# Two GpSimd drains left out at the end of a graph network, and the wait for the last outputs behind a flag load

## The chip, the cores and the metric

The kernel runs on one core of one Trainium2 chip. The metric is device time in microseconds (us) of one execution. The profile is of one execution; its span runs from the first recorded instruction to the last, and the device time of the same execution is a little longer. Engines are called PE (TensorE), DVE (VectorE), ACT (ScalarE), POOL (GpSimd) and SP (SyncE).

## The reference

Two graph networks over 6250 nodes of 64 features and 200,000 edges, each added to its input and followed by a layer normalisation:

```
edge_index = jnp.stack([src, dst])
x = _layernorm(x + sage(sage(x) -> relu))          # mean over incoming edges, two layers
x = _layernorm(x + L1(x, src, dst, edge_attr_16))  # three message layers, batch norm between them
```

```
m   = concatenate([x[dst], x[src], edge_attr]) @ W.T + b
agg = segment_sum(m, dst, num_segments=n)
h   = relu(agg)            # after layers 0 and 1: relu(batchnorm(h))
```

The output is `out`, 6250 rows of 64 float32 values.

## The kernel before

The kernel first builds a dense count matrix of the edges (`build`), and then, in `layers`, multiplies node features by it five times. Each of these propagations is one call of `propagate` with p = 0 to 4, inside a block of its own; after p = 2 and p = 3 a second block holds the batch normalisation. A propagation works through 13 blocks of nodes (NB, 512 nodes each, the last one short). For each of them PE sums in PM (L1325), DVE scales into S and F, PE applies the weights (PH, L1543 and L1544) and turns the result (PG, L1570). In p = 4 DVE then adds it to R and normalises it (`norm`, L1636 to L1645) into the tile `dd`, and POOL writes `dd` to `out` with one DMA for each of the 13 (`write`, L1474 and, for the last, L1477). The DMAs count up two semaphores in turn, `s_o[0]` and `s_o[1]` (named o0 and o1 in the program, numbers 196 and 197), by 16 each.

Order within an engine is the order in which the code is written. Between the engines there are semaphores inside a block, and a barrier of all five engines at each block's end. In the barrier each of PE, DVE, ACT and SP executes a drain and adds one to a gather semaphore; POOL executes a drain of its own, waits until four have been gathered, and then adds four to a release semaphore for which the others wait. All of this has the line of the `with nc.Block()`: L1001 for the propagations, L1035 for the last block.

At the end of p = 4 POOL waits until all its output DMAs have landed:

```
        if p == 4:
            g.wait_ge(s_o[0], 16 * 7)
            g.wait_ge(s_o[1], 16 * 6)
```

The closing block (from L1035) is a fallback. During p = 4 DVE has written a one-word `flag` (L1731), which says whether the count matrix was trustworthy. Each engine loads it into a register (`value_load`: L1038 on SP, L1046 on POOL, L1054 on DVE, L1062 on PE, L1070 on ACT) and branches. With the flag at 0, as here, each jumps over the code of the whole slow path (a second version of everything, `slow`) to the barrier that ends the closing block, and the program is over. `propagate` is also called for parts of this slow path, with its parameter `block` an object of class `Stage`, and then its variable `slow` is true.

Of the kernel before, what the change touches and what calls it, by code (L numbers as in the profile page):

```python
# [205 lines left out]
def blk(b):  # L206
    return 512 if b < NB - 1 else LASTW
# [36 lines left out]
def gnn(nc, ins, out):  # L244
    ctx = ExitStack()
    with ctx:
# [40 lines left out]
        }  # L287
        build(nc, ins, m)
        layers(nc, ins, m, out)


# [644 lines left out]
def layers(nc, ins, m, out):  # L936
    ctx = ExitStack()
    with ctx:
        def sb(name, shape, dt=f32):
            return ctx.enter_context(nc.sbuf_tensor(name, shape, dt))  # L940

        def ps(name, shape, dt=f32):
            return ctx.enter_context(nc.psum_tensor(name, shape, dt))

        def sem(name):
            return ctx.enter_context(nc.semaphore(name))

        t = {
            "Ares": m["Ares"],
            "Aring": m["Aring"],  # L950
            "S": sb("S", [128, 2, 512]),
            "rc": sb("rc", [128, 2, 512]),
            "cnt": sb("cnt", [16, NP // 16]),
            "hT": sb("hT", [128, 2, 512]),
            "dd": sb("dd", [128, 2, 4, 64]),
            "sq": sb("sq", [128, 2, 4, 64]),
            "st": sb("st_", [128, 2, 4, 4]),
            "bst": sb("bst", [64, NB, 6]),
            "bag": sb("bag", [64, 8]),
            "PM": [ps(f"PM{i}", [128, 512]) for i in range(3)],  # L960
            "PH": [ps(f"PH{i}", [128, 512]) for i in range(2)],
            "PG": [ps(f"PG{i}", [128, 4, 128]) for i in range(2)],
            "PB": ps("PB", [64, 512]),
            "gi": sb("gi", [128, 1], i32),
            "gd": sb("gd", [128, 1], i32),
            "gf": sb("gf", [128, 1]),
            "msg": sb("msg", [128, 64]),
            "junk": sb("junk", [128, 13 * SW // 4], u8),
            "dsum": sb("dsum", [128, 8, 4]),
            "csum": m["csum"],  # L970
            "s_sr": [sem(f"s_sr{i}") for i in range(len(SUMS))],
            "s_rb": [sem(f"s_rb{i}") for i in range(len(FACTORS))],
            "s_fin": sem("s_fin"),
            "s_xp": [sem(f"s_xp{i}") for i in range(len(GIVEN))],
            "fl": sb("fl", [1, 16]),

            "s_ar": [[sem(f"s_ar{i}_{h}") for h in range(2)] for i in range(2)],
            "s_mm": sem("s_mm"),
            "s_ea": sem("s_ea"),
            "s_cl": sem("s_cl"),  # L980
            "s_cr": sem("s_cr"),
            "s_cd": sem("s_cd"),
            "s_ck": sem("s_ck"),
            "s_xt": sem("s_xt"),
            "s_bp": sem("s_bp"),
            "s_again": sem("s_again"),
            "s_rd": sem("s_rd"),
        }


        t["acc"] = t["hT"][:].rearrange("p a b -> p (a b)").bitcast(u16)[:, 0:13 * SW // 2]
        sets = [{}, {}, {}]

        def pick(k):
            def get(name):
                if name not in sets[k]:
                    sets[k][name] = sem(f"q{k}_{name}")
                return sets[k][name]
            return get
        for p in range(5):  # L1000
            with nc.Block() as block:  # L1001
                if p == 0:
                    setup(nc, ins, m, t, list, block)
                propagate(nc, ins, m, t, p, pick(p % 2), out, lambda: [*sets[1 - p % 2].values()], block)
            if p in (2, 3):
                with nc.Block() as block:
                    normalise(nc, m, t, p, pick(p % 2), block)
        once = [x for x in t.values() if type(x) is type(t["s_mm"])]
        slow = [*restart(nc, ins, m, t, [*sets[0].values(), *sets[1].values(), *once]), Stage()]
        general(nc, ins, m, t, -1, pick(2), slow[-1])  # L1010
        slow.append(Stage())
        setup(nc, ins, m, t, lambda: list(sets[2].values()), slow[-1])
        for p in range(5):
            slow.append(Stage())
            general(nc, ins, m, t, p, pick(2), slow[-1])
            slow.append(Stage())
            propagate(nc, ins, m, t, p, pick(p % 2), out,
                      lambda p=p: [*sets[2].values(), *sets[1 - p % 2].values()], slow[-1])
            if p in (2, 3):
                slow.append(Stage())  # L1020
                normalise(nc, m, t, p, pick(p % 2), slow[-1])
        s_meet, s_go = sem("s_meet"), sem("s_go")

        def meet(engine, k):

            if engine is nc.gpsimd:
                engine.drain()
                engine.wait_ge(s_meet, 4 * (k + 1))
                engine.sem_inc(s_go, 1)
            else:  # L1030
                engine.drain().then_inc(s_meet, 1)
                engine.wait_ge(s_go, k + 1)
                engine.drain()

        with nc.Block() as block:  # L1035
            @block.sync
            def _(sp):
                wrong = sp.value_load(m["flag"][0:1, 0:1], min_val=0, max_val=1)  # L1038
                with sp.If(wrong == 1):
                    for k, part in enumerate(slow):  # L1040
                        part.run_sync(sp)
                        meet(sp, k)

            @block.gpsimd
            def _(g):
                wrong = g.value_load(m["flag"][0:1, 0:1], min_val=0, max_val=1)  # L1046
                with g.If(wrong == 1):
                    for k, part in enumerate(slow):
                        part.run_gpsimd(g)
                        meet(g, k)  # L1050

            @block.vector
            def _(v):
                wrong = v.value_load(m["flag"][0:1, 0:1], min_val=0, max_val=1)  # L1054
                with v.If(wrong == 1):
                    for k, part in enumerate(slow):
                        part.run_vector(v)
                        meet(v, k)

            @block.tensor  # L1060
            def _(pe):
                wrong = pe.value_load(m["flag"][0:1, 0:1], min_val=0, max_val=1)  # L1062
                with pe.If(wrong == 1):
                    for k, part in enumerate(slow):
                        part.run_tensor(pe)
                        meet(pe, k)

            @block.scalar
            def _(act):
                wrong = act.value_load(m["flag"][0:1, 0:1], min_val=0, max_val=1)  # L1070
                with act.If(wrong == 1):
                    for k, part in enumerate(slow):
                        part.run_scalar(act)
                        meet(act, k)
# [255 lines left out]
def propagate(nc, ins, m, t, p, sem, out, past, block):  # L1330
# [4 lines left out]
    conv, slow = p - 2, type(block) is Stage  # L1335
# [117 lines left out]
    @block.gpsimd  # L1453
    def _(g):
        if past():
            g.dma_reset()
            for used in past():
                g.sem_clear(used)

        def hand_over(b):  # L1460

            n = blk(b)
            if b >= 2:
                g.wait_ge(s_g if p == 1 else s_h, b - 1)
            nc.gpsimd.memset(S[64:128, b % 2, 0:n], 0.0).then_inc(s_t1, 1)
            g.dma_start(S[0:64, b % 2, 0:n], m["agg"][:, b * 512:b * 512 + n]).then_inc(s_t2, 16)
            g.wait_ge(s_t1, b + 1)
            g.wait_ge(s_t2, 16 * (b + 1))
            g.sem_inc(s_ok, 1)

        def write(b):
            g.wait_ge(s_gd, b + 1)
            if b < NB - 1:
                g.dma_start(out[b * 512:(b + 1) * 512, :].rearrange("(j q) f -> q j f", q=128),  # L1474
                            dd[:, b % 2]).then_inc(s_o[b % 2], 16)
            else:
                g.dma_start(out[b * 512:N, :], dd[0:TAIL, b % 2, 0]).then_inc(s_o[b % 2], 16)  # L1477

        for b in range(NB + 3):
            if b < NB and slow:  # L1480
                hand_over(b)
            if p == 4 and b >= 3:
                write(b - 3)
        if p == 4:
            g.wait_ge(s_o[0], 16 * 7)
            g.wait_ge(s_o[1], 16 * 6)

# [507 lines left out]
```

## Time and profile before

| what | us |
|---|---|
| median of 3 executions | 1168.31 |
| lowest and highest | 1167.57, 1171.08 |
| the profiled execution, device time | 1168.37 |
| its span | 1166.6 |
| outside its span | 1.8 |
| last output DMA begins on POOL | 1157.1 |
| last instruction of the span | 1166.5 |

PE is busy for 90% of the span, and the chain of work that ended last runs over its matmuls until the last ten microseconds. Those ten hold only semaphore, load, branch and drain instructions, which the profile's page doesn't count as busy; they can be read under their lines, with engine names such as POOLq and DVEq. In such a row the first number after the "x" and count is the duration in nanoseconds (minimum, median, maximum), then come the start of the first and of the last in us.

### The profile page before, as it was taken

The page shows a single profiled execution, that of the slowest core. Times are in us where ns is not written, and L with a number is a line of the kernel's source. Part 1 is how long each engine was busy: PE and PEld are TensorE (multiplying, and loading weights), DVE is VectorE, ACT ScalarE, POOL GpSimd, SP SyncE. Part 2 cuts the span into 40 slices and gives each one's busy share as a digit, 9 for nine tenths or more (in the row PEclk, how much of TensorE's full clock was granted, in tenths as well). Part 3 has the DMA queues.
Part 4 walks back from the last instruction along what each step waited for, and adds up shares of the span by engine and source line. Part 5 has one row for each costly group of instructions (what it writes and reads, how often), then busy time and mean ns, then how long its engine had stood idle before and what let it go on. Part 6 is the DMA issues. An engine that isn't in the chain of part 4 may idle for free. (4 is left out here: it accounts for less than half of the span.)

```text
span 1166.6 us, 21101 instructions
## 1 busy us (share of the span) xinstructions
PE 1052.0 (90%) x8433; PEld 655.3 (56%) x8433; DVE 711.7 (61%) x1415; ACT 368.6 (32%) x733; POOL 108.5 (9%) x125
## 2 busy tenths in 40 slices
PE   0259999999999997999999999998989998999993
PEld 0248988989999984545555444444434444444442
DVE  5798989899899853623433755544464554334434
ACT  2475667776676530200000110113320204200000
POOL 4122222232211110000000000000000000000001
PEclk9768988989898898999999999998989998999996
DMA  6325546546455338983685526665026665037740
GB/s 163 54 73 190 182 127 216 195 142 224 131 176 166 109 151 270 417 282 120 266 319 180 227 84 270 241 248 221 14 100 254 255 234 221 19 136 282 285 170 22
DMA packets 67310, 216.89 MB, mean 186 GB/s; under 512 B 32176, under 2 KB 45227, under 8 KB 53667
## 3 DMA queue, kind: packets, MB, share of 16 engines
q1 hardware_dynamic: 59188, 164.51, 39.7%
q0 software_dynamic: 8016, 50.95, 12.1%
q8 instruction: 68, 1.11, 0.4%
q14 instruction: 38, 0.31, 0.1%
HBM read 170.68 MB, written 44.74 MB: 185 GB/s over the span
## 5 line engine op out<-in xcount | busy, mean ns | idle before, releaser
L1325 PE MATMUL PM<-Aring,Xop 128*128 128x512 fp8e4 (+1 forms) x1960 | 399.8, 364 | 0.0
L1325 PEld LDWEIGHTS PM<-Aring,Xop 128*128 128x128 f16 x1960 | 181.7, 98 | 218.5 <-issue 18.7
L1850 ACT ACTIVATE F<-PH,bag 64x512 f32<-64x512 f32 (+1 forms) x39 | 25.5, 658 | 374.8 <-PE PH L1544 374.7
L1325 PE MATMUL PM<-Ares,Xop 128*128 128x512 fp8e4 x588 | 136.2, 386 | 2.9 <-ACT Xop L1889 1.4
L773 PE MATMUL PW<-Aring 128*128 128x52 fp8e4 (+3 forms) x2151 | 114.7, 216 | 18.3 <-ACT F L837 16.9
L773 PEld LDWEIGHTS PW<-Aring 128*128 128x128 fp8e4 x2151 | 110.5, 103 | 21.5 <-ACT F L837 18.5
L786 PE MATMUL PA<-Ares,ea 128*128 128x32 f16 x1867 | 112.3, 235 | 0.0
L786 PEld LDWEIGHTS PA<-Ares,ea 128*128 128x128 f16 x1867 | 108.4, 116 | 0.0
L1683 DVE TENSOR_SCALAR S<-PM 128x256 f32<-128x256 f32 (+1 forms) x75 | 31.3, 418 | 114.9 <-PE PM L1325 97.2
L1325 PEld LDWEIGHTS PM<-Ares,Xop 128*128 128x128 f16 x588 | 55.8, 99 | 70.5 <-issue 7.4
L837 ACT ACTIVATE F<-PW 128x392 uint16<-128x392 f32 x196 | 85.0, 508 | 6.0 <-PE PW L773 3.7
L748 PE MATMUL PX<-Xop 128*128 128x256 fp8e4 (+1 forms) x588 | 76.3, 299 | 1.1 <-ACT Ares L852 1.1
L1474 POOL DMA_DIRECT2D out<-dd x12 | 9.1, 754 | 708.7 <-DVE dd L1645 708.7
L630 DVE TENSOR_TENSOR Aring<-Ares 128x4096 uint16<-128x4096 uint16 x31 | 70.8, 2284 | 6.2 <-PE PW L773 5.8
L748 PE MATMUL PX<-Aring,Xop 128*128 128x256 fp8e4 x539 | 68.3, 292 | 2.5 <-ACT Ares L852 2.5
L748 PEld LDWEIGHTS PX<-Xop 128*128 128x128 f16 x588 | 62.5, 110 | 13.3 <-issue 1.6
L1713 DVE TENSOR_TENSOR hT<-hT,Aring 128x1536 uint16<-128x1536 uint16 (+2 forms) x71 | 67.6, 952 | 2.3
L637 DVE TENSOR_TENSOR Aring<-Ares 128x1144 uint16<-128x1144 uint16 (+22 forms) x139 | 67.2, 546 | 0.0
L748 PEld LDWEIGHTS PX<-Aring,Xop 128*128 128x128 f16 x539 | 56.3, 105 | 12.4 <-DVE Xop L655 2.6
L1681 DVE TENSOR_TENSOR S<-PM,rc 128x256 f32<-128x256 f32 (+1 forms) x25 | 9.3, 413 | 77.0 <-PE PM L1325 64.3
L726 PE MATMUL PT<-ident,Ares 128*128 128x128 f32 x32 | 8.7, 365 | 49.5 <-ACT Ares L803 48.4
L1644 DVE RECIPROCAL st_<-st_ 128x4 f32<-128x4 f32 (+1 forms) x26 | 4.6, 177 | 76.0 <-ACT st_ L1809 72.5
(154 smaller groups left out, 1159.8 us busy)
## 6 DMA issues: line engine op xcount, KB each, us to landing
Aring<-adj SPq DMA_DIRECT2D x72, 1568.0 KB, 9.8
adj<-Aring POOLq DMA_DIRECT2D x12, 1568.0 KB, 6.1
adj<-Xop POOLq DMA_DIRECT2D x12, 1568.0 KB, 6.6
Ares<-adj SPq DMA_DIRECT2D x6, 1568.0 KB, 22.0
rc<-ea_sum SPq DMA_DIRECT2D x36, 128.0 KB, 5.7
eaf<-in_erow SPq DMA_DIRECT2D x62, 51.0 KB
Aring<-adj SPq DMA_DIRECT2D x4, 784.0 KB, 4.4
rc<-rc_d SPq DMA_DIRECT2D x12, 256.0 KB, 10.3
```

Source lines behind the costliest of these rows:

```text
L630: nc.vector.tensor_tensor(lo[:, h % 2].rearrange("p s (i j e) -> p s i j e", i=8, e=2), At[:, t % 2, at:at + HS].rearrange("p s i (o e) -> ...
L637: last = nc.vector.tensor_tensor(key[:, o:o + 26 * n].rearrange("p (q v e) -> p q v e", v=26, e=2), Dv[:, t % 2, d, i:i + n].rearrange("p ...
L748: last = nc.tensor.matmul(PX[:, 0:n], m["Xop"][0][:, h, :], of[:, h, :], start=h == 0, stop=h == NT - 1)
L773: last = nc.tensor.matmul(PW[begun % RING][:, c:c + 52 * (z - y)].rearrange("p (d v b) -> p d v b", d=z - y, b=2), lo[:, h % 2, i, :].bitc ...
L786: last = nc.tensor.matmul(PA[st % 2][:, w % 8 * PD:w % 8 * PD + PD], ea_flat[:, c % 4, i * 33:i * 33 + 128], ohd[:, c % 4, :, i], start=j ...
L837: nc.scalar.activation(to, PW[g % RING][:, 0:416].rearrange("p (q h) -> p h q", h=52)[:, 0:NT], ACT.Copy, scale=32.0).then_inc(s_wev, 1)
L1325: last = nc.tensor.matmul(o, x[:, h, :], rhs, start=h == 0, stop=h == NT - 1)
L1474: g.dma_start(out[b * 512:(b + 1) * 512, :].rearrange("(j q) f -> q j f", q=128), dd[:, b % 2]).then_inc(s_o[b % 2], 16)
L1681: last = nc.vector.tensor_tensor(part, of, natural(by), ALU.mult)
L1683: own(nc.vector.tensor_single_scalar(part, of, 1 / CS, ALU.mult))
L1713: own(nc.vector.tensor_tensor(to[:, 0:h1 - h0], to[:, 0:h1 - h0], of[:, h0:h1], ALU.add))
L1850: nc.scalar.activation(F[0:64, c:c + w], PH[b % 2][0:64, 0:w], ACT.Relu, bias=t["bag"][:, 4 + conv:5 + conv]).then_inc(s_hr, 1)
```

## The change

Two blocks are built with `no_gpsimd_drain`: that of p = 4 and the closing one. In the barrier that ends such a block POOL has no drain. The other four engines have, in place of the one drain that waits for the release semaphore to be 0 and then counts up the gather semaphore, a plain drain and then a semaphore instruction that does this: one instruction more for each of the four, in each of the two barriers. The two waits of POOL for the outputs are taken out of the end of p = 4 (but kept in the slow path's copy of it), and stand in the closing block between POOL's flag load and its branch.

```
-            with nc.Block() as block:
+            with nc.Block(no_gpsimd_drain=p == 4) as block:
                 if p == 0:
                     setup(nc, ins, m, t, list, block)
                 propagate(nc, ins, m, t, p, pick(p % 2), out, lambda: [*sets[1 - p % 2].values()], block)
...
-        with nc.Block() as block:
+        with nc.Block(no_gpsimd_drain=True) as block:
...
             def _(g):
                 wrong = g.value_load(m["flag"][0:1, 0:1], min_val=0, max_val=1)
+                for i in range(2):
+                    g.wait_ge(sets[0][f"o{i}"], 16 * (7 - i))
                 with g.If(wrong == 1):
...
-        if p == 4:
+        if p == 4 and slow:
             g.wait_ge(s_o[0], 16 * 7)
             g.wait_ge(s_o[1], 16 * 6)
```

On POOL, from the last outputs of p = 4 to the branch of the closing block, the program has this order before (q0_o0 and q0_o1 are the two output semaphores, the rows on L1001 and L1044 are jumps to a block's end and into the closing block; drains and bare semaphore instructions are not listed, a wait stands with the next listed row):

```order
L1474 DMA out<-dd 128x4x64 [waits q0_gd] x12
L1477 DMA out<-dd 106x64 [waits q0_gd]
L1001 UNCONDITIONAL_BRANCH [waits q0_o1,q0_o0]
L1044 UNCONDITIONAL_BRANCH [waits barrier_Pool_Activation_PE_DVE_SP_gather]
L1046 TENSOR_LOAD flag
L1046 ISA x2
L1047 COMPARE_AND_BRANCH
```

And this is the same stretch of POOL in the changed kernel, whose line numbers are two higher behind the edits:

```order
L1476 DMA out<-dd 128x4x64 [waits q0_gd] x12
L1479 DMA out<-dd 106x64 [waits q0_gd]
L1001 UNCONDITIONAL_BRANCH
L1044 UNCONDITIONAL_BRANCH [waits barrier_Pool_Activation_PE_DVE_SP_gather]
L1046 TENSOR_LOAD flag
L1046 ISA x2
L1049 COMPARE_AND_BRANCH [waits q0_o1,q0_o0]
```

The waits for the two output semaphores have gone from the jump ahead of the barrier to the branch that ends POOL's part of the closing block. On every engine all that stands ahead of the end of p = 4 is as it was.

## Rows read from the trace of the kernel before

**Rows 1.** The page's first line.

```profile
span 1166.6 us, 21101 instructions
```

**Rows 2.** Chain that ended last, window 1155 to 1170: start us, us, what.

```profile
1156.59 0.23 DVE dd L1645
1156.82 0.28 issue
1157.11 0.59 POOL out L1477
```

**Rows 3.** Busy time by stretch; columns as in its heading.

```profile
core 0: us, PE busy (x) PEld busy (x) DVE busy (x) ACT busy (x) POOL busy (x), PEclk, DMA share, GB/s
1157.10:1158.90 1.80, 0.00 (x0) 0.00 (x0) 0.00 (x0) 0.00 (x0) 0.59 (x1) 0.50 0.05 15
1161.80:1166.30 4.50, 0.00 (x0) 0.00 (x0) 0.00 (x0) 0.00 (x0) 0.00 (x0) 0.50 0.09 22
```

**Rows 4.** Line 1477, the last output: its row and its landing.

```profile
L1477 POOL DMA_DIRECT2D out<-dd x1: 590/590/590, 1157.1 to 1157.1; - x1
...
DMA to landing us min/median/max: 1.8/1.8/1.8
```

**Rows 5.** Line 1486, POOL's wait for o1 at the end of p = 4.

```profile
L1486 POOLq EVENT_SEMAPHORE  x1: 17/17/17, 1157.5 to 1157.5; - x1
```

**Rows 6.** Line 1001, window 1150 to 1170: the barrier that ends p = 4.

```profile
L1001 POOLq EVENT_SEMAPHORE  x2: 17/17/17, 1160.2 to 1160.3; - x2
...
L1001 DVEq DRAIN  x1: 258/258/258, 1156.6 to 1156.6; - x1
L1001 POOLq COMPARE_BRANCH  x1: 47/47/47, 1158.9 to 1158.9; - x1
L1001 POOLq DRAIN  x1: 1122/1122/1122, 1159.1 to 1159.1; - x1
...
L1001 DVEq EVENT_SEMAPHORE  x1: 21/21/21, 1160.4 to 1160.4; - x1
```

**Rows 7.** Line 1001 over the whole span: POOL's drains in five barriers.

```profile
L1001 POOLq DRAIN  x5: 34/40/8812, 448.8 to 1159.1; - x5
```

**Rows 8.** Tile flag: who writes it, and two of the five loads.

```profile
L1731 DVE TENSOR_SCALAR flag<-fl x1: 141/141/141, 1103.9 to 1103.9; 1x1 int32<-1x1 f32 x1
L1046 POOLq TENSOR_LOAD <-flag x1: 512/512/512, 1160.4 to 1160.4; - x1
...
L1054 DVEq TENSOR_LOAD <-flag x1: 547/547/547, 1160.5 to 1160.5; - x1
```

**Rows 9.** Lines 1047, 1039, 1055, 1063, 1071: the five branches of the closing block.

```profile
L1047 POOLq COMPARE_BRANCH  x1: 50/50/50, 1161.2 to 1161.2; - x1
...
L1039 SPq COMPARE_BRANCH  x1: 57/57/57, 1161.2 to 1161.2; - x1
...
L1055 DVEq COMPARE_BRANCH  x1: 76/76/76, 1161.7 to 1161.7; - x1
...
L1063 PEldq COMPARE_BRANCH  x1: 3577/3577/3577, 1161.4 to 1161.4; - x1
...
L1071 ACTq COMPARE_BRANCH  x1: 45/45/45, 1161.2 to 1161.2; - x1
```

**Rows 10.** Line 1035: the barrier that ends the program.

```profile
L1035 POOLq EVENT_SEMAPHORE  x2: 17/17/17, 1166.4 to 1166.5; - x2
L1035 ACTq DRAIN  x1: 72/72/72, 1164.4 to 1164.4; - x1
L1035 PEldq DRAIN  x1: 72/72/72, 1165.0 to 1165.0; - x1
L1035 SPq DRAIN  x1: 72/72/72, 1165.1 to 1165.1; - x1
L1035 POOLq DRAIN  x1: 110/110/110, 1165.2 to 1165.2; - x1
L1035 DVEq DRAIN  x1: 59/59/59, 1166.3 to 1166.3; - x1
```

**Rows 11.** DMA queues, window 1162 to 1165: packets, MB, share.

```profile
q14 instruction: 5, 0.04, 6.7%
q8 instruction: 1, 0.02, 2.5%
```

More of the change, by code:

```diff
@@ L1000, in layers @@
         for p in range(5):
-            with nc.Block() as block:
+            with nc.Block(no_gpsimd_drain=p == 4) as block:
                 if p == 0:
@@ L1033, in meet @@
                 engine.drain()
-        with nc.Block() as block:
+        with nc.Block(no_gpsimd_drain=True) as block:
             @block.sync
@@ L1046, in _ @@
                 wrong = g.value_load(m["flag"][0:1, 0:1], min_val=0, max_val=1)
+                for i in range(2):
+                    g.wait_ge(sets[0][f"o{i}"], 16 * (7 - i))
                 with g.If(wrong == 1):
@@ L1483, in _ @@
                 write(b - 3)
-        if p == 4:
+        if p == 4 and slow:
             g.wait_ge(s_o[0], 16 * 7)
```

## The prediction, made before the changed kernel ran

> **What bounds the kernel now.** I read the page's head first, then the chain of waits near its end, then the last ten microseconds line by line, since the change touches nothing ahead of them. The span is 1166.6 us [rows 1]. The chain of work ends with DVE's last normalisation step and POOL's last output at 1157.1 [rows 2]. The reader is to see that 9.5 us of span follow in which no engine computes: in the stretches from there on all busy columns are zero but for POOL's 0.59 [rows 3]. What these 9.5 us consist of has to be followed through sequencer rows:
>
> - POOL issues the last output at 1157.1, and it lands 1.8 us later, at 1158.9 [rows 4]. POOL's sequencer is already at its first wait at 1157.5 [rows 5], so from then on it only waits for data.
> - At 1158.9 its jump to the block's end goes through, at 1159.1 its drain begins and takes 1.122, at 1160.2 it finds the four others gathered and at 1160.3 it releases them [rows 6]. DVE, the last of the others, had drained at 1156.6 for 0.258. So the release at 1160.3 hangs on POOL alone.
> - All load the flag at 1160.4 to 1160.5 [rows 8] and reach their branches at 1161.2 (POOL, SP, ACT), 1161.4 (PE) and 1161.7 (DVE) [rows 9].
> - They arrive at the closing barrier at 1164.4 (ACT), 1165.0 (PE), 1165.1 (SP), 1165.2 (POOL) and 1166.3 (DVE) [rows 10]. From branch to arrival that is 3.2, 3.6, 3.9, 4.0 and 4.6 us. The only transfers in this stretch are of instructions, six packets [rows 11]: the jump over the slow path is paid by fetching code, and for PE the branch itself is recorded as 3.577 long.
> - POOL sees the fourth arrival at 1166.4, 0.1 behind DVE's, and the span ends 0.2 later.
>
> So three waits follow each other: the landing, POOL's drain, and DVE's code fetch.
>
> **The change part by part.**
>
> *The two waits and the first drain.* Both leave the path to the release. Before, release = 1160.3. After it, POOL is free at 1157.5 [rows 5]; the jump to the next instruction takes 0.2 (1158.9 to 1159.1) and from gather to release it is 0.1 (1160.2 to 1160.3) [rows 6]: 1157.5 + 0.2 + 0.1 = 1157.8. Gain 2.5. The others are no new wait, since DVE had drained by 1156.6 + 0.26 = 1156.9. Bounds: if the jump only starts when the DMA instruction has run its 0.59 to 1157.7 [rows 4], the release is at 1158.0 and the gain 2.3; if the jump costs its own 0.047 alone, it is at 1157.65 and 2.65. I take 2.5, since the wait at 1157.5 is a row of the very same spot.
>
> *The waits in their new place.* The flag load begins 0.1 behind the release and the branch stands 0.8 behind that (1160.4 to 1161.2 [rows 8, 9]): 1157.9 + 0.8 = 1158.7. The output lands at 1158.9, so POOL waits 0.2. Queued behind is only its own jump to the last barrier, 4.0 as before: POOL arrives at 1162.9. DVE, shifted by 2.5, arrives at 1163.8. The wait has 0.9 of cover. If the outputs landed more than 0.9 later than now, each further microsecond would cost one. The flag is no hazard: it was written at 1103.9 [rows 8].
>
> *The closing drain.* POOL's 0.110 at 1165.2 lies beside DVE's fetch until 1166.3 [rows 10]. Worth nothing.
>
> *The extra semaphore instructions.* One per engine and barrier. In the first barrier all four are long early. In the closing one DVE's stands on the path; the rows of such instructions are 0.017 to 0.021 [rows 6], and from one to the next on POOL it is 0.1. Cost 0.02 to 0.1; I take 0.05.
>
> *The fetch after the branch.* It is not touched by the diff, so I shift it rigidly: nothing gained, nothing lost. That is a choice. The bounds come from the five engines' own times: DVE's 4.6 could become ACT's 3.2, and then POOL's arrival at 1162.9 would be last, 0.9 earlier; or another engine could take what DVE took, for PE 1158.9 + 4.6 = 1163.5, still below DVE's 1163.8, so on that side I keep the difference between neighbours, 0.7 (DVE 4.6, SP 3.9), as loss.
>
> The Trainium skill (Runtime: NRT & Kernel Launch, section Instruction fetch mechanics) says that code is fetched ahead in sequence only, and that a taken branch to a target outside the two pages held waits for a DMA of the page. The trace agrees: 3.2 to 4.6 us from branch to arrival with instruction packets between [rows 9 to 11]. By that rule the wait begins with the branch, so it shifts with it.
>
> *Sum.* 2.5 − 0.05 = 2.45. The profiled execution took 1168.37 in all, 1.8 more than its span; with that part unchanged it would be 1168.37 − 2.45 = 1165.92. The median of the runs, 1168.31, is 0.06 lower: 1165.9 in round numbers, 0.21% less.
>
> **The rivals.**
>
> *A, rigid shift:* 1165.9, as above.
>
> *B, the drain's time comes back on POOL.* Of POOL's five drains at propagation barriers three took about 0.04, but the one in which it had just issued DMAs took 1.122 and another 8.812 [rows 7]: it is not a fixed price but the end of some work on POOL, here until 1160.2. If the flag load needs that work to be over, it starts at 1160.2, POOL branches at 1161.0 and arrives 4.0 later at 1165.0, behind DVE's 1163.8. The end is then at 1165.0 + 0.1 + 0.2 = 1165.3, a gain of 1.3: 1167.0. For it: PE's and ACT's drains don't show such a thing. Against it: loads take 0.512 on POOL and 0.547 on DVE alike, as if the sequencer did them alone, and POOL's wait at 1157.5 passed while its DMA instruction still ran. A variant in which the release itself waits for that work gains nothing: 1168.3.
>
> *C, the fetch gets shorter.* The five engines fetch together, and POOL's fetch now comes 0.2 later than in a rigid shift. If DVE's then takes what POOL's or ACT's takes, it is 0.6 to 1.4 earlier, and POOL at 1162.9 cuts the rest off: gain 3.05 to 3.35, time 1165.0 to 1165.3. For it: nothing in the program makes DVE's jump longer. Against it: DVE branches last, 0.3 to 0.5 behind the others, and that stays.
>
> *D, the end of the program is fetched twice (slower).* Place: the barrier of the closing block, on PE, DVE, ACT or SP. The two added instructions push the barrier's last ones on. If on one engine they now fall behind the end of the fetched piece, it waits for a second fetch before it can arrive: 3.2 to 4.6 us against the gain of 2.45, so 0.75 to 2.15 slower: 1169.1 to 1170.5. It decides as soon as the second fetch takes more than 2.5. For it: packets come in pieces of 0.04 MB / 5 = 8 KB and one of about 16 KB [rows 11]. Against it: only two instructions move, and a piece holds many; four engines make four chances. The same page and section of the Trainium skill names blocks of 16 KiB or 256 instructions; by that, an estimate is 4 × 2 in 256, about 3 in 100.
>
> **How the numbers follow.** A 0.63, C 0.17, B 0.12 (the variant without gain 0.03 of it), D 0.05, and 0.03 for something that I do not see on either side. About 0.3%, or 3.5 us, is what a measurement of this kernel tells from no change; so faster means below 1164.8, slower above 1171.8. A alone scatters by the fetch (+0.7, −0.9) and by the median of runs that lay between 1167.57 and 1171.08: its own range is 1164.8 to 1167.2. Faster: a tenth of A and six tenths of C, 0.17. Slower: D with a disturbed median, and half of the unseen: 0.03. The rest, 0.80, is no measurable change, though the trace should show a gain. The range from 1164.5 to 1168.5 holds A, B and nearly all of C.
>
> **What would show it.** Release at about 1157.8 instead of 1160.3, flag loads at 1157.9, no drain of POOL in either barrier; POOL's branch at 1158.9, on the landing; DVE last at the closing barrier at 1163.8; span 1164.1 and still 1.8 outside. A load on POOL that ends after 1160.5 shows B; a DVE arrival less than 4.2 behind its branch shows C; an arrival more than 6 behind its branch shows D. The forecast is wrong if the release stays behind 1158.9, or if time outside the span grows by what the span loses.

## The result, and the profile after

| | before | changed kernel |
|---|---|---|
| median of 22 executions each | 1167.61 | 1165.08 |
| lowest and highest | 1163.64, 1171.08 | 1161.28, 1167.85 |
| profiled execution, device time | 1168.37 | 1167.65 |
| its span | 1166.6 | 1165.9 |
| issue of the last output to the end of the span | 9.5 | 7.1 |

The ratio is 0.9966, 95% interval 0.9954 to 0.9979: the change makes the kernel faster by 2.5 to 5.4 us. The forecast, 1165.9 or a ratio of 0.9979, had the direction and lies on the interval's weak edge, but it gave "no measurable change" a chance of 0.80, and that was wrong.

Executions of one kernel differ by 2.0 to 3.5 us (standard deviation), and in the profiles most of the difference lies ahead of the last output: its issue came at 1157.1 and 1160.1 in two profiles of the kernel before and at 1161.0 in one of the changed kernel, with the same code up to there. So spans say little. What I compare is the *tail*, from the issue of the last output on POOL to the end of the span. In the changed kernel's page this issue stands at 1158.7, and its landing is late (line 1479, its row and its landing, against [rows 4]):

```profile
L1479 POOL DMA_DIRECT2D out<-dd x1: 592/592/592, 1158.7 to 1158.7; - x1
DMA to landing us min/median/max: 4.3/4.3/4.3
```

The barrier that ends p = 4 (line 1001, from 1150 on) answers to [rows 6]. Each x2 row is the arrival and the release:

```profile
L1001 DVEq EVENT_SEMAPHORE  x2: 21/21/21, 1158.5 to 1158.9; - x2
L1001 POOLq EVENT_SEMAPHORE  x2: 17/17/17, 1158.7 to 1158.8; - x2
...
L1001 DVEq DRAIN  x1: 258/258/258, 1158.2 to 1158.2; - x1
```

POOL releases at 1158.8, 0.07 behind the issue; before it was 3.2 behind. The drain and the wait are gone, and no other engine has become the last. Then the flag load on POOL, POOL's branch, PE's branch and DVE's branch (lines 1046, 1049, 1065 and 1057, against [rows 8, 9]):

```profile
L1046 POOLq TENSOR_LOAD <-flag x1: 511/511/511, 1158.9 to 1158.9; - x1
...
L1049 POOLq COMPARE_BRANCH  x1: 54/54/54, 1163.0 to 1163.0; - x1
...
L1065 PEldq COMPARE_BRANCH  x1: 4851/4851/4851, 1160.0 to 1160.0; - x1
...
L1057 DVEq COMPARE_BRANCH  x1: 76/76/76, 1160.2 to 1160.2; - x1
```

POOL's load takes 0.511 as before, so the drain's time did not come back there. But its branch stands until 1163.0, on the late landing. The last barrier (line 1035) answers to [rows 10]:

```profile
L1035 POOLq EVENT_SEMAPHORE  x2: 17/17/17, 1165.7 to 1165.8; - x2
L1035 ACTq DRAIN  x1: 78/78/78, 1163.7 to 1163.7; - x1
L1035 SPq DRAIN  x1: 63/63/63, 1163.9 to 1163.9; - x1
L1035 DVEq DRAIN  x1: 71/71/71, 1164.4 to 1164.4; - x1
L1035 PEldq DRAIN  x1: 72/72/72, 1164.9 to 1164.9; - x1
```

The four others are there by 1165.1; POOL comes at 1165.7. DVE, last by 1.1 us before, is now third, 4.2 behind its branch instead of 4.6.

### The profile page after: what moved, and what is told of

It is laid out like the page before. It is cut to its first block and busy times, and to the rows that moved or that the text cites. A ratio compares the mean times of both kernels' runs of the same rounds, so it can differ in the third digit from the quotient of the medians.

```text
span 1165.9 us, 21106 instructions
## 1 busy us (share of the span) xinstructions
PE 1051.6 (90%) x8433; PEld 654.8 (56%) x8433; DVE 711.9 (61%) x1415; ACT 368.7 (32%) x733; POOL 108.7 (9%) x125
## 3 DMA queue, kind: packets, MB, share of 16 engines
q8 instruction: 69, 1.13, 0.4%
```

## The experiments

Times below are us behind the issue of the last output, in the one profiled execution of each kernel; "DVE's jump" is from its branch to its arrival at the last barrier.

| kernel | release | landing | POOL's branch | DVE's jump | last to arrive | tail |
|---|---|---|---|---|---|---|
| before | 3.2 | 1.8 | 4.1 | 4.6 | DVE | 9.5 |
| before, again | 3.2 | 1.8 | 4.1 | 4.5 | DVE | 9.4 |
| before, DVE +1 | 3.2 | 1.8 | 4.1 | 4.0 | DVE | 8.8 |
| waits moved, drains kept | 2.5 | 1.8 | 3.4 | 4.5 | DVE | 8.7 |
| drains out, waits kept | 2.05 | 1.8 | 2.9 | 4.2 | DVE | 8.0 |
| changed | 0.07 | 4.3 | 4.3 | 4.2 | POOL | 7.1 |
| changed, second | 0.07 | 2.6 | 2.7 | 3.7 | POOL | 5.6 |
| changed, third | 0.07 | 3.1 | 3.1 | 3.8 | PE | 6.6 |
| changed, all engines hold | 0.07 | 2.8 | 2.8 | 3.6 | PE | 7.6 |
| changed, waits behind the branch | 0.07 | 2.8 | 1.0 | 3.9 | DVE | 5.7 |
| changed, DVE +64 | 0.07 | 1.8 | 1.8 | 3.9 | DVE | 5.4 |
| one barrier less | none | 2.4 | 0.8 | 3.8 | DVE | 4.9 |
| one barrier less, DVE +64 | none | 2.3 | 0.8 | 3.1 | POOL | 4.0 |

**Controls.** Both kernels once more.

> The kernel before, once more, as a control: ratio 1.000 within the interval, and a second look at its tail. If the tail (issue of the last output to the end of the span) is a property of the program it is 9.5 us within 0.3, with the landing 1.8 us behind the issue and POOL's drain at 1.1; if DVE's long fetch was chance, the tail is up to 1 us shorter.

> The changed kernel, once more. If the late landing comes from the program's code fetches, it is again over 3 us behind the issue and POOL is again last at the closing barrier, tail 7.1 within 0.3; if it was chance, the landing is at 1.8, and the tail 6.4 to 6.8. The time by the tail alone: 2.4 us or 0.2% less than before; a saving beyond the tail, elsewhere in the program, would show as a ratio below 0.9970.

> The changed kernel, a third look at its tail. Two executions had the last landing at 4.3 and 2.7 us behind the issue and a tail of 7.1 and 5.6. If the lateness is the program's and only its size scatters, the landing is again later than 2.4 and the tail between 5.5 and 7.2; a landing at 1.8 would speak for chance alone.

Before again: ratio 0.9991 (0.9967 to 1.0014), tail 9.4, drain 1.122. Changed again: ratio 0.997 (0.995 to 0.999), tail 5.6; third profile (one execution, 1165.51 us): 6.6. The landing came at 2.6 in the second, between the two values expected, and at 3.1 in the third. So the tail before is 9.4 to 9.5 in both its profiles; that of the changed kernel scatters from 5.6 to 7.1, mean 6.5, a gain of 3.0 us or 0.25%. That lies inside both measured intervals, so no saving elsewhere is needed, though the intervals don't exclude one.

**Each half alone.** The first kernel has only the `no_gpsimd_drain` edits, the second only the moved waits:

```
-            with nc.Block() as block:
+            with nc.Block(no_gpsimd_drain=p == 4) as block:
...
-        with nc.Block() as block:
+        with nc.Block(no_gpsimd_drain=True) as block:
```

> The two GpSimd drains are left out, POOL's wait for the outputs stays ahead of the barrier. Measured from the issue of the last output on POOL to the end of the span, before had 9.5 us and the changed kernel 7.1. Theory 1 (a chain of landing, drain, code fetch): the landing stays at 1.8 behind the issue, the release comes some 0.25 later at 2.05 instead of 3.2, and the tail is 9.5 - 1.1 = 8.4 us, about 0.1% of the time. Rival (the drain's 1.12 us is work that POOL has to finish anyway): the flag load on POOL takes 1.6 us instead of 0.5, and the tail is over 9.0.

> The waits for the outputs stand behind POOL's flag load as in the changed kernel, but POOL's drains in both barriers are kept. Theory 1 with a drain of fixed length (1.1 us): release 1.4 us behind the issue of the last output, tail 9.5 - 1.8 = 7.7. Rival: the drain waits for what POOL has handed out, so it ends at the same 3.1 us behind the issue as before, whatever stands ahead of it, and the tail stays at 9.5; then the gain needs both edits together.

Drains out alone: ratio 0.9987 (0.9967 to 1.0008), tail 8.0; release 2.05 as expected. The tail is 0.4 shorter than expected, because DVE's jump took 4.2 instead of 4.6. Waits moved alone: ratio 0.9998 (0.9979 to 1.0018), tail 8.7: neither theory. POOL's drain (line 1001) and the last output's landing (line 1479) there:

```profile
L1001 POOLq DRAIN  x1: 2360/2360/2360, 1160.7 to 1160.7; - x1
```

```profile
L1479 POOL DMA_DIRECT2D out<-dd x1: 592/592/592, 1160.7 to 1160.7; - x1
DMA to landing us min/median/max: 1.8/1.8/1.8
```

It is neither 1.12 long nor over at 3.1, but takes 2.36 from the moment of issue. With the wait ahead of it, it ended at 3.1 [rows 4, 6]. So a drain of POOL right behind an output costs 2.4 by itself; the wait of 1.8 hid some of that. The two halves save 0.7 (waits) and 1.15 (drains) at the release when done alone, and 3.1 together: the first to go exposes the other.

**Where POOL waits, and for what.** In the first, POOL's waits follow its branch; in the second all engines wait for the landing before they branch (the same lines on SP, DVE, PE and ACT):

```
                 wrong = g.value_load(m["flag"][0:1, 0:1], min_val=0, max_val=1)
-                for i in range(2):
-                    g.wait_ge(sets[0][f"o{i}"], 16 * (7 - i))
                 with g.If(wrong == 1):
+                    for i in range(2):
+                        g.wait_ge(sets[0][f"o{i}"], 16 * (7 - i))
...
+                for i in range(2):
+                    g.wait_ge(sets[0][f"o{i}"], 16 * (7 - i))
```

```
                 wrong = sp.value_load(m["flag"][0:1, 0:1], min_val=0, max_val=1)
+                for i in range(2):
+                    sp.wait_ge(sets[0][f"o{i}"], 16 * (7 - i))
```

> The changed kernel, with POOL's two waits moved once more, behind its branch and so behind its jump over the slow path. In the changed kernel POOL's branch waited for the last output's landing until 4.3 us behind the issue, and POOL was the last at the closing barrier. Theory 2 (POOL's fetch now stands in line behind a late landing): POOL branches about 1.0 us behind the issue, arrives before 5.5, and PE's arrival at 6.35 sets the end: tail 6.7 instead of 7.1. Rival (the fetches end together whatever POOL does): tail 7.1 within 0.2.

> The changed kernel, but all five engines wait for the outputs' landing between their flag load and their branch. No code is fetched while the last output is written. Theory 2 (the code fetches of the other four, which now start 1.2 us behind the issue, hold up the last packets of the output): the landing is back at 1.8 us behind the issue instead of 4.3, all branch at about 2.0, and the tail is 2.0 + 4.6 + 0.3 = 6.9, no longer than that of the changed kernel. Rival (the landing is late because the drain is gone, or by chance): landing near 4.3, all branches behind it, and a tail of 9 or more.

Waits behind the branch: ratio 0.9974 (0.9949 to 0.9999), tail 5.7. POOL branches at 1.0, has jumped by 4.9, finds the outputs landed and is no longer last. The tail is 1.0 shorter than expected, since PE arrived at 5.2 and not at 6.35. All hold: ratio 0.9984 (0.9962 to 1.0005), tail 7.6 where 6.9 was expected, since the landing was still 2.8. That speaks against the fetches that follow the branches as the cause: none had begun. But the trace shows one instruction packet beside the output. These are the queues of that kernel from the issue (1162.57) on for 1.79 us, the time a landing took before:

```profile
q0 software_dynamic: 30, 0.03, 5.3%
q14 instruction: 1, 0.01, 2.0%
```

In the same window before there are 32 packets of the output and none of instructions; here two of the 32 are missing. In the second profile of the changed kernel all 32 have begun by then, and yet the landing is at 2.6:

```profile
q0 software_dynamic: 32, 0.03, 5.5%
q14 instruction: 1, 0.01, 1.4%
issues: line engine op xcount, KB each, median us to landing
out<-dd POOLq DMA_DIRECT2D x1, 26.5 KB, 2.6
```

The landing is counted complete with the last of 16 increments of the output's semaphore. In six of the seven late profiles 15 of them came by 1.8, as before, and only one was late (at 4.3 two were). The recorded packets had ended 0.6 to 1.3 us ahead of that last increment, against 0.35 where nothing was late. What happens in between is not shown.

**One instruction's position on DVE.** Which engine fetches there? In the kernel before, DVE has a gap behind its flag load (line 1054: load from 1160.5 for 0.547, next at 1161.4); in the changed kernel (line 1056) the gap stands ahead of the load:

```profile
L1054 DVEq FUSED_REGOPS  x1: 213/213/213, 1161.4 to 1161.4; - x1
```

```profile
L1056 DVEq TENSOR_LOAD <-flag x1: 540/540/540, 1159.3 to 1159.3; - x1
L1056 DVEq FUSED_REGOPS  x1: 212/212/212, 1159.9 to 1159.9; - x1
```

Released at 1158.9, DVE loads only at 1159.3, where POOL loaded at 1158.9; then it goes on without a gap. The 0.4 us have moved by one instruction, and DVE's barrier has one instruction more. So a piece of DVE's code ends right here. Two kernels test that: one instruction more on DVE in the kernel before, and 64 more, early in p = 4, in the changed one:

```
+        if p == 4 and not slow:
+            v.sem_inc(t["s_pad"], 1)
```

```
                 tell(i)
+                if 2 <= i < 6:
+                    for _ in range(16):
+                        v.sem_inc(t["s_pad"], 1)
```

> The kernel before with one more semaphore instruction on DVE, at DVE's end of p = 4, where DVE waits for POOL anyway; drains and waits as before. Theory 3 (position): DVE's code crosses from one fetched piece into the next right at its flag load; in the kernels that keep the drains the crossing stands behind the load, so the fetch ahead that it starts is still running when DVE branches, and the target's fetch takes 1.6 us (landed pieces at other times take 0.3 to 0.6). One instruction more, as the changed kernel has on DVE, puts the crossing ahead of the load: then the gap of 0.39 us moves from behind the load to ahead of it, the last fetch takes about 0.5, DVE goes from branch to arrival in 3.6 to 4.2 instead of 4.5 us, and the tail (issue of the last output to the end of the span) is 8.5 to 8.9 instead of 9.4. Rival (the longer fetch belongs to the barrier's form, not to the position): tail 9.4, gap behind the load.

> The changed kernel with 64 more semaphore instructions on DVE, 16 each in four of the long waits early in p = 4, off the path. They move DVE's crossing between two fetched pieces away from the flag load. Theory 2 and 3 together: no instruction packet runs beside the last output, the landing is back at 1.8 us behind the issue (changed kernel 4.3 and 2.7), DVE's gap of 0.4 ahead of its load goes, POOL branches at 1.8, and the tail is 5.0 to 5.4 instead of 5.6 and 7.1. Rival (the late landing comes from the branches' fetches, which stay): landing at 2.5 or later, tail 5.6 or more.

Before with one more: tail 8.8. DVE's load, branch (lines 1055 and 1056) and arrival (line 1036):

```profile
L1055 DVEq TENSOR_LOAD <-flag x1: 544/544/544, 1165.5 to 1165.5; - x1
L1055 DVEq FUSED_REGOPS  x1: 213/213/213, 1166.1 to 1166.1; - x1
```

```profile
L1056 DVEq COMPARE_BRANCH  x1: 76/76/76, 1166.4 to 1166.4; - x1
```

```profile
L1036 POOLq DRAIN  x1: 113/113/113, 1170.1 to 1170.1; - x1
L1036 DVEq DRAIN  x1: 64/64/64, 1170.4 to 1170.4; - x1
```

The gap has moved ahead of the load, the jump takes 4.0 instead of 4.5 to 4.6. Both are what the changed kernel shows, with drains and waits as before. The time, 1.0007 (0.999 to 1.0025), does not resolve 0.6 us. With 64 more the jump in the changed kernel meets no other fetch of DVE's, and the landing (line 1480) and POOL's branch (line 1050) are:

```profile
L1480 POOL DMA_DIRECT2D out<-dd x1: 590/590/590, 1151.9 to 1151.9; - x1
DMA to landing us min/median/max: 1.8/1.8/1.8
```

```profile
L1050 POOLq COMPARE_BRANCH  x1: 54/54/54, 1153.7 to 1153.7; - x1
```

Its queues for 1.79 us from the issue (1151.92) on, without any instruction packet:

```profile
DMA packets 32, 0.03 MB, mean 15 GB/s; under 512 B 17, under 2 KB 32, under 8 KB 32
## 3 DMA queue, kind: packets, MB, share of 16 engines
q0 software_dynamic: 32, 0.03, 5.6%
```

Tail 5.4, ratio 0.9977 (0.9961 to 0.9993). Over all thirteen profiles of the table the landing is at 1.8 in the six without an instruction packet in that window, and at 2.3 to 4.3 in the seven with one or two. Five of the six have their release so late that no fetch could fall there; the test of the cause is the sixth, the kernel with 64 more, and it is one execution. Its tail is not clearly shorter than the changed kernel's, which was 5.6 once.

**One barrier less.** The closing block's code is put at the end of p = 4's block, so that each engine loads the flag and jumps as soon as its own work is done:

```
+            def fall_back(engine, name):
+                if engine is not nc.vector:
+                    engine.wait_ge(t["s_flag"], 1)
+                wrong = engine.value_load(m["flag"][0:1, 0:1], min_val=0, max_val=1)
+                with engine.If(wrong == 1):
...
+                if engine is nc.gpsimd:
+                    for i in range(2):
+                        engine.wait_ge(sets[0][f"o{i}"], 16 * (7 - i))
...
+                propagate(nc, ins, m, t, p, pick(p % 2), out, lambda: [*sets[1 - p % 2].values()], block)
+                if p == 4:
+                    closing(block)
```

> The changed kernel without the barrier between p = 4 and the closing block: a semaphore tells the other engines that the flag is written, each loads it and jumps over the slow path as soon as its own part of p = 4 is done, and POOL waits for the outputs behind its jump; one barrier ends the program. (Inside the slow path an added meeting of all engines takes the old barrier's place.) If the code fetch is what the tail consists of, SP, PE and ACT have fetched before the last output is issued. DVE ends 0.2 behind its last step and arrives at 0.5 + 4.6 = 5.1 us or less behind the issue, POOL at 0.8 + 4.0 = 4.8: tail 5.2 to 5.5 instead of 7.1, some 4 us or 0.35% under before. Rival: fetches in the middle of p = 4 hold up its own instructions or its outputs, and the gain is below 3 us.

> The kernel without the barrier between p = 4 and the closing block, with the same 64 semaphore instructions on DVE. DVE's gap of 0.4 ahead of its branch goes and its fetch starts that much sooner: tail 4.4 to 4.7 instead of 4.9, in all some 4.8 us or 0.4% under before. Rival: a fetch elsewhere takes the place, tail 4.9 or more.

Ratio 0.9965 (0.9941 to 0.9988), tail 4.9; with DVE's 64 instructions 0.9969 (0.9951 to 0.9987), tail 4.0. Both tails are below what was expected, the first because DVE's jump took 3.8 and not 4.6. The branches of the first (line 1032):

```profile
L1032 SPq COMPARE_BRANCH  x1: 58/58/58, 1133.0 to 1133.0; - x1
L1032 PEldq COMPARE_BRANCH  x1: 3857/3857/3857, 1150.7 to 1150.7; - x1
L1032 ACTq COMPARE_BRANCH  x1: 45/45/45, 1157.7 to 1157.7; - x1
L1032 DVEq COMPARE_BRANCH  x1: 76/76/76, 1158.3 to 1158.3; - x1
L1032 POOLq COMPARE_BRANCH  x1: 59/59/59, 1158.4 to 1158.4; - x1
```

PE pays its 3.9 us of jump ahead of the last output. Both kernels beat the kernel before, with medians of 1164.25 against 1170.30 and 1163.46 against 1168.18; that they beat the changed one is shown for the tail (4.0 and 4.9, one execution each, against 5.6 to 7.1), not by the times, whose intervals overlap.

## Why the prediction was right and where it was wrong

- *Three waits follow each other:* right. Both edits were needed: alone they shorten the tail by 0.8 (waits) and 1.5 us (drains), and neither is told from no change by its time. The six instruction packets of [rows 11] are those up to 1165; five more follow between 1165 and 1167.
- *POOL free at 1157.5, release at 1157.8, gain 2.5:* **this is the term that was mis-sized.** The row at 1157.5 [rows 5] is not POOL becoming free. It is a wait for semaphore o1, that is, for the twelfth output, and that output was issued at 1155.06 and landed 2.4 later, at 1157.5 (line 1474, from 1154 to 1156, kernel before):

```profile
L1474 POOL DMA_DIRECT2D out<-dd x1: 750/750/750, 1155.1 to 1155.1; - x1
...
DMA to landing us min/median/max: 2.4/2.4/2.4
```

  POOL stood free from the issue on. The release came 0.07 behind it, not 0.7: the gain there is 3.1, outside my bounds of 2.3 to 2.65.
- *The flag load does not need the drained work (against rival B):* right, 0.511.
- *The moved wait has 0.9 of cover:* wrong. I held the landing at 1.8 although the change brings code fetches to within 1.3 us of the issue, and it came at 2.6 to 4.3. POOL was last in two of three profiles, by 0.6 and 0.2 us (in the third it was PE). It would have been worse with the 4.0 that I took for POOL's own jump: in these two profiles it took 2.7 and 2.8. The prediction names this case with its price but gave it no chance.
- *The fetch shifts rigidly:* wrong in part. DVE's jump fell from 4.5 or 4.6 to 3.7 to 4.2. This is rival C in its effect, for a reason that I had denied ("nothing in the program makes DVE's jump longer"): one instruction's position did, as the kernel with one more shows.
- *Rival D, an added instruction that pushes code past the end of a piece, in the closing barrier:* no engine arrived there more than 4.9 behind its branch, so it did not happen. An end of a piece was near, but at DVE's flag load, and it was the instruction added in the first barrier that moved it, with the opposite sign.
- *The closing drain is worth nothing, the extra semaphore instructions cost 0.02 to 0.1:* right for what they take themselves. From DVE's last drain to POOL's gathering event it is 0.17 in the changed kernel with 64 more, where DVE is last, and 0.09 before. What the one in DVE's first barrier did by its position was not in the sum.

In sum: 0.6 at the release and 0.4 to 0.9 at DVE's jump were missing, the late landing and PE's longer branch took 0.2 to 1.1 back: 3.0 on average instead of 2.45. That is 0.25% and would not by itself pass the 0.3% that I held to be the least measurable. The measured 0.34% does, and what it has beyond the tails lies inside its interval. The 0.80 for "no measurable change" failed by that bound: with 22 executions each the interval was ±0.13%, so that even the forecast 0.21% would have been clear of no change.

Open: why in two of three profiles of the changed kernel a second packet of queue q8, by its time PE's, came at 2.4 us and PE's branch took 4.8 or 4.9 instead of 3.5, with the same code (in both it also began 0.17 later, at 1.30 instead of 1.13); why DVE's fetch behind its own fetch ahead is so slow (1.6 us in the three profiles with a jump of 4.5 to 4.6); what holds up the last increment of the late landings; and what a POOL drain waits for beyond the landing.

## What to carry to other kernels

A row of a wait that passes at some time says when its event came, not when the engine was free: look up which semaphore it waits for and when that event happened, before taking it as the engine's first free moment. Where a program ends in code that jumps far, count the jump as a transfer (2.5 to 4.9 us here) that can start early, and that can hold up a small transfer that it meets. When a wait is removed, check each transfer that now runs beside another, and give the case a chance.

## What the runs showed of the hardware that I had not expected

- A drain on POOL issued right behind an output DMA took 2.36 us; 1.95 us behind it, with the output landed, it took 1.122; at three earlier barriers, where POOL had issued no DMA since a drain 2 us before, about 0.04 [rows 7].
- With one or two packets of instructions beside it, a 26.5 KB output landed 0.5 to 2.5 us later than the 1.8 without; at most four of its 32 packets were late, and one or two of its 16 semaphore increments.
- A jump over the slow path took 3.2 to 4.9 us on PE, DVE, ACT and SP when all jumped together. In the kernel with one barrier less SP jumps alone, from 1133.0 to 1135.5: 2.5 us; PE, also alone there, took 3.9.
- The Trainium skill (Runtime: NRT & Kernel Launch, section Instruction fetch mechanics) says that crossing into the next piece in sequence is mostly hidden. Here DVE showed a gap of 0.4 us at the place taken to be such a crossing, and a jump 0.3 us behind the gap took 4.5 to 4.6 us instead of 4.0.
